# Float32r pairs against scaled fp16 pairs in a fused latent-attention layer: scores, queries, latent and feed-forward products

## The reference

```python
xn = _layernorm(x)
q = (xn @ wq).reshape(b, s, 16, 192)                 # 128 plain and 64 rotary columns per head
kva = xn @ wkv_a                                     # 128 latent and 64 rotary columns
ckv = ckv * rsqrt(mean(ckv * ckv) + 1e-6) * kv_norm_scale
kv = (ckv @ wkv_b).reshape(b, s, 16, 256)            # 128 key and 128 value columns per head
q_pe, k_pe = _rope(q_pe, cos, sin), _rope(k_pe, cos, sin)
scores = einsum('bhqd,bhkd->bhqk', qs, ks) * 192 ** -0.5     # causal
out = softmax(scores) @ v @ wo
x = x + out + einsum('btd,rde->bte', xn, factors) / sqrt(8) + bias
```

## Time and profile before

| | |
|---|---|
| median of 3 runs | 1624.83 us (1623.87 to 1628.01) |
| profiled execution, its own time | 1624.0 us |
| its span in the profile | 1622.2 us |
| TensorE busy, share of the span | 1578.3 us, 97% |
| VectorE | 984.7 us, 61% |
| ScalarE | 875.5 us, 54% |
| GpSimd | 902.1 us, 56% |
| granted TensorE clock, mean | 0.992 |

### The profile page before, as it was taken

One profiled execution on the slowest core, in us unless ns is written; L12 is line 12 of the kernel. 1 busy time (PEld: TensorE's weight loads), 2 busy tenths in 40 slices (PEclk: granted clock), 3 DMA queues, 4 the chain that ended last, 5 costly groups with the idle time before them and its releaser, 6 DMA issues.

```text
span 1622.2 us, 24924 instructions
## 1 busy us (share of the span) xinstructions
PE 1578.3 (97%) x7856; PEld 1198.7 (74%) x7856; DVE 984.7 (61%) x2286; ACT 875.5 (54%) x2264; POOL 902.1 (56%) x856
## 2 busy tenths in 40 slices
PE   5789999999999999999999999999999999999998
PEld 5667777777777777677777777777777777778786
DVE  6765666566666655655555555555656656665766
ACT  4554555555555556556555555555535555543554
POOL 3664556455555555555655655566645555563553
PEclk9899999999999999999999999999999999999999
DMA  8855878878787879778888778787957778865675
GB/s 279 307 127 120 172 164 166 178 149 178 149 167 164 162 177 225 154 174 167 165 179 163 152 150 164 167 209 160 242 131 166 165 167 169 216 166 123 168 177 127
DMA packets 646882, 280.23 MB, mean 173 GB/s; under 512 B 599392, under 2 KB 612192, under 8 KB 645344
## 3 DMA queue, kind: packets, MB, share of 16 engines
q1 hardware_dynamic: 646752, 278.63, 76.7%
HBM read 102.37 MB, written 33.55 MB: 84 GB/s over the span
## 4 chain that ended last, share of the span: by engine, by line
PE 92%; DVE 3%; ACT 2%; POOL 1%; issue 1%; DMA 1%; SPq 0%; ACTq 0%; POOLq 0%; DVEq 0%
PE ps L318 18%; PE ps L320 17%; PE ps L319 17%; PE ps L442 8%; PE ps L447 8%; PE ps L448 8%; PE ps L444 8%; PE ps L443 8%; POOL q L1022 1%; ACT ex L622 1%; DVE kt L803 1%; DMA wsq<-wq_in 0%; PE ps L337 0%; DMA st<-x_in 0%; DVE acc L896 0%
## 5 line engine op out<-in xcount | busy, mean ns | idle before, releaser
L1031 POOL TENSOR_TENSOR st<-ex,st 128x512 f16<-128x512 f32 (+3 forms) x640 | 639.7, 1020 | 617.6 <-ACT st L632 613.1
L622 ACT ACTIVATE ex<-ps,nm 128x512 f32<-128x512 f32 (+3 forms) x640 | 395.4, 621 | 639.8 <-DVE nm L869 639.8
L632 ACT ACTIVATE st<-ex 128x512 f16<-128x512 f32 (+3 forms) x640 | 344.5, 566 | 6.4 <-ACT ex L622 0.8
L853 DVE TENSOR_REDUCE gm<-ps 128x1 f32<-128x512 f32 (+1 forms) x384 | 248.8, 667 | 130.4 <-PE ps L448 130.1
L442 PE MATMUL ps<-kTh,q 128*128 128x512 f32 (+3 forms) x640 | 250.0, 391 | 4.2 <-DVE kRl L817 3.8
L447 PE MATMUL ps<-kRh,q 128*128 128x512 f32 (+3 forms) x640 | 232.8, 364 | 4.9 <-POOL q L1022 4.9
L444 PE MATMUL ps<-kTh,q 128*128 128x512 f32 (+3 forms) x640 | 232.3, 363 | 0.0
L443 PE MATMUL ps<-kTl,q 128*128 128x512 f32 (+3 forms) x640 | 231.7, 362 | 0.0
L448 PE MATMUL ps<-kRl,q 128*128 128x512 f32 (+3 forms) x640 | 231.7, 362 | 0.0
L318 PE MATMUL ps<-pT,vH 128*128 128x512 f16 (+3 forms) x640 | 223.5, 349 | 0.0
L319 PE MATMUL ps<-pT,vH 128*128 128x512 f16 (+3 forms) x640 | 222.1, 347 | 0.0
(11 more groups left out here) (144 smaller groups left out, 2446.4 us busy)
## 6 DMA issues: line engine op xcount, KB each, us to landing
wA<-w_abs SPq DMA_DIRECT2D x48, 512.0 KB, 3.8
wV<-w_vo SPq DMA_DIRECT2D x48, 512.0 KB, 3.7
wP<-w_pe SPq DMA_DIRECT2D x24, 512.0 KB, 4.1
pT<-st SPq DMA_TRANSPOSE x640, 3.3
w_abs<-wA SPq DMA_DIRECT2D x16, 512.0 KB, 2.9
w_vo<-wV SPq DMA_DIRECT2D x16, 512.0 KB, 3.0
x_t<-early SPq DMA_DIRECT2D x3, 2048.0 KB, 8.5
xT<-x_t SPq DMA_DIRECT2D x6, 1024.0 KB, 7.6
```

The source lines that it names most:

```text
L622: e.activation(ex[:, n % NEX, 0:keys], s_bank(n)[:, 0:keys], ACT.Exp, bias=nm[:, (i * QT + r) % 4:(i * QT + r) % 4 + 1], scale=SCALE, accu ...
L632: e.activation(stage(n, keys)[:, :, 0, :], ex[:, n % NEX, 0:keys].rearrange("p (t n) -> p t n", n=P), ACT.Copy).then_inc(z["a_pH"], 1)
L853: e.tensor_reduce(m, b, AX_X, ALU.max).then_inc(z["v_max"], 1)
L1031: e.tensor_tensor(s[:, :, 1, :], ex[:, n % NEX, 0:keys].rearrange("p (t n) -> p t n", n=P), s[:, :, 0, :], ALU.subtract).then_inc(z["g_pL" ...
```

## The change

- The parts of x, W_abs, the rotary weights, the latent weights, the keys, the queries and the factor sum become fp16 instead of float32r. The transposes, the product W_abs itself, W_vo and the output product stay float32r or float32.
- So that small low parts are not lost in fp16, operands carry powers of two: x by 2^10 (through the normalisation), keys by 2^12 (through the latent scale), queries are multiplied by 2^-14 when they are read from PSUM (L605: `scale=BACK`, an immediate), the rotary tables by 2^-14 on the host.
- Each pair of heads gets a weight scale of its own, worked out on the chip (`squares`, `scale_pair`): VectorE squares and sums Wq (1024 columns), the rotary weights (512) and Wk (256) of two heads, TensorE adds the partitions with a matrix of ones (`nrm`, 4 columns), VectorE makes a reciprocal square root out of an integer formula and from it four columns of `scales`. The latent weights (`nra`) and the factor sum (`nrf`) get one each.
- The scale of the exponentials (L622) was the immediate `SCALE` and is now the pointer `scales[:, pair(i), 2:3]`; likewise in `row_max`, `w_pe`, `w_abs`, the latent and feed-forward products.
- Order: `squares(i + 2)` in r0 of even units up to 12, `scale_pair(i + 2)` and the rotary weights' high part in r1, their low part in r2. `nrm` takes a bank in the turn, right ahead of `tq`. Key and value weights now have buffers and loads of their own, two heads at once. The factor sum is squared in r0 of unit 0, split in r1, and its eight feed-forward tiles lie in r2 and r3 instead of in r0 to r3; the bias is added by GpSimd within unit 0.
- Stores and reloads of W_abs, the rotary weights, x and the factor sum have half the bytes.

The diff, cut to its core:

```diff
-HEADROOM = float(np.log(32.0))
+XS, KS, WS, PS, BACK = 2.0 ** 10, 2.0 ** 12, 2.0 ** 15, 2.0 ** 15, 2.0 ** -14
+HEADROOM = float(np.log(PS))
...
     if r == 0:
-        for e in range(2, H, 2):
-            if i == max(0, e - 3):
-                out.append(("wpe", e))
         if 1 <= i <= H:
             out.append(("wo", i - 1))
         if i + 1 < NU:
             out.append(("q", i + 1))
-        if i + 2 <= H + 2:
-            out.append(("skv", i + 2))
+        if 3 <= i + 2 <= H + 2:
+            out.append(("sv", i + 2))
+        if i % 2 == 0 and i + 2 < H:
+            out.append(("sq", i + 2))
+        if i == 0:
+            out.append(("sqf", 0))
...
-    if i == 0:
-        out += [("ffn", n) for n in range(2 * QT) if min((n + 1) // 2, 3) == r]
+    if i == 0 and r >= 2:
+        out += [("ffn", n) for n in range((r - 2) * QT, (r - 1) * QT)]
...
     if r == 1:
+        if i % 2 == 0 and i + 2 < H:
+            out += [("nrm", i + 2), ("wpe", i + 2)]
+        if i == 0:
+            out.append(("nf", 0))
...
-IN_BANKS = ("q", "pe", "tkv", "wvo", "tq", "wabs", "out", "ffn")
+IN_BANKS = ("q", "pe", "tkv", "wvo", "tq", "wabs", "out", "ffn", "nrm", "nf")
...
-        kTh = sb("kTh", [P, S], F32R)
+        kTh = sb("kTh", [P, S], F16)
...
             def wq_transpose(h):
                 b = free_bank(("tq", h))
-                e.wait_ge(z["d_wq"], 16 * (h + 1))
+
+                e.wait_ge(z["v_sq"], h // 2 + 1)
...
+            def norm(key, ready, columns):
+
+                b = free_bank(key)
+                e.wait_ge(z[ready], count(key))
+                e.matmul(b[:, 0:columns.shape[-1]], ones[:, :], columns, start=True, stop=True).then_inc(
+                    z["p_" + key[0]], 1)
...
-                             bias=nm[:, (i * QT + r) % 4:(i * QT + r) % 4 + 1], scale=SCALE,
+                             bias=nm[:, (i * QT + r) % 4:(i * QT + r) % 4 + 1], scale=scales[:, pair(i), 2:3],
                              accum_out=ssum[:, i % 2, r, p:p + 1]).then_inc(z["a_exp"], 1)
...
+            def factors_high():
+                e.wait_ge(z["v_fsc"], 1)
+                e.activation(ff[:, 0, :, :], fsum, ACT.Identity, bias=eps[:, 2:3], scale=fsc[:, 1:2]).then_inc(
+                    z["a_ff"], 1)
...
+            def square_sum(w, at, n, total):
+                return e.tensor_tensor_reduce(out=sqr[:, at:at + n], in0=w, in1=w, scale=1.0, scalar=0.0, op0=ALU.mult,
+                                              op1=ALU.add, accum_out=total)
...
+            def squares(i):
+
+                e.wait_ge(z["d_wk"], 16 * (i + 2))
+                e.tensor_tensor(wsk[:, :, :], wsk[:, :, :], scl[:, 0:1].unsqueeze(2).broadcast_to([P, 2, P]),
+                                ALU.mult).then_inc(z["v_sk"], 1)
...
+                square_sum(wsq[:, :, :, :].rearrange("p a k n -> p (a k n)"), 0, 2 * E, nrm[:, 0:1])
+                e.wait_ge(z["d_wp"], 64 * (i // 2 + 1))
+                square_sum(wsp[:, :, :].rearrange("p k n -> p (k n)"), 2 * E, E, nrm[:, 1:2])
+                e.wait_ge(z["v_sk"], i // 2 + 1)
+                square_sum(wsk[:, :, :].rearrange("p a n -> p (a n)"), 3 * E, 2 * P, nrm[:, 2:3]).then_inc(z["v_sq"], 1)
...
             def q_latent(i):
                 e.wait_ge(z["a_q"], i + 1)
-                e.tensor_tensor(q[:, i % 2, 1, :], bank(("q", i)), f(q[:, i % 2, 0, :]), ALU.subtract).then_inc(
-                    z["v_q"], 1)
+                e.scalar_tensor_tensor(out=q[:, i % 2, 1, :], in0=bank(("q", i)), scalar=BACK, in1=q[:, i % 2, 0, :],
+                                       op0=ALU.mult, op1=ALU.subtract).then_inc(z["v_q"], 1)
...
-            for k4 in range(KE):
-                e.wait_ge(z["a_ff"], k4 + 1)
-                e.tensor_tensor(ff[:, 1, k4, :], fsum[k4], f(ff[:, 0, k4, :]), ALU.subtract).then_inc(z["v_ff"], 1)
```

More of the change, by code:

```diff
@@ L115, in fills @@
             out.append(("parts", i + 1))
+    if r == 2 and i % 2 == 0 and i + 2 < H:
+        out.append(("wpe_low", i + 2))
     for e in range(2, NU, 2):
@@ L127, in fills @@
             out.append(("parts", i + 1))
+    if i == 0:
+        out += [("bias", n) for n in range(2 * QT) if min((n + 1) // 3, 2) == r]
+    for k in range(2, NC):
+        if i == k * H + 1:
+            out.append(("bias", k * QT + r))
     return out
-IN_BANKS = ("q", "pe", "tkv", "wvo", "tq", "wabs", "out", "ffn")
+IN_BANKS = ("q", "pe", "tkv", "wvo", "tq", "wabs", "out", "ffn", "nrm", "nf")
 def bank_order():
-    pre = [("tq", 0), ("tkv", 0)]
+    pre = []
     for t in range(NT + 4):
@@ L322, in count @@
             def count(key):
-                return key[1] // 2 + 1 if key[0] == "pe" else key[1] + 1
+                return key[1] // 2 + 1 if key[0] in ("pe", "nrm") else key[1] + 1
             def free_bank(key):
@@ L593, in w_pe @@
                     e.wait_ge(z["d_sP"], 16 * (i // 2))
-                e.activation(by4(wP[:, 0, :]), wsp[:, :, :], ACT.Copy).then_inc(z["a_wpe"], 1)
+                e.activation(by4(wP[:, 0, :]), wsp[:, :, :], ACT.Identity, bias=eps[:, 2:3],
+                             scale=scales[:, i // 2, 1:2]).then_inc(z["a_wpe"], 1)
             def w_o(h):
@@ L868, in row_max @@
                     e.wait_ge(z["a_exp"], rows_done(R - 4))
-                e.scalar_tensor_tensor(out=nm[:, R % 4:R % 4 + 1], in0=m, scalar=-SCALE, in1=head[:, 0:1],
+                if i < H and r == 0:
+                    e.wait_ge(z["v_scale"], i // 2 + 1)
+                e.scalar_tensor_tensor(out=nm[:, R % 4:R % 4 + 1], in0=m, scalar=scales[:, pair(i), 3:4], in1=head[:, 0:1],
                                        op0=ALU.mult, op1=ALU.add).then_inc(z["v_nm"], 1)
@@ L1222, in _ @@
             load_wo(0)
-            load_wkv(2)
-            load_wq(2)
+            for m in range(2, 4):
+                load_wk(m)
+                load_wq(m)
+            load_wp(2)
+            load_wv(3)
             store_abs(0)
```

363 lines of the change are left out of this document (224 added, 139 removed).

## The result

The changed kernel takes 1650.38 us (1646.57 to 1651.71, four runs) against 1624.35 for the kernel before: ratio 1.0153, 95% interval 1.0128 to 1.0177, so 26 us slower. The forecast was 1638 (1622 to 1652 for its own case, 1606 to 1664 in all). The profiled execution took 1651.7 us with a span of 1649.8, 27.6 more than the span before. One execution of each of two later runs took far longer than all others (3208 us with the pointer in the kernel before, 2258 us with the factor in the queries) and is left out of their ratios.

The account below looks back on a forecast made before the run. TensorE was taken as the bound, with little to spare. Terms -69 + 45 + 7 + 16.5 + 13.7 + 1 = +14 on 1624.0 us gave 1638 us (1622 to 1652 for its own case, 1606 to 1664 in all).

Parts of the forecast that it names:

- The even units of chunk 3: Units 2 to 12: squares on VectorE and a bank wait stall TensorE 7.5 us in each of six: 45 us.
- Both waits: Even units of chunk 3: r1's bias waits behind squares, then the key transpose for the bank of r1's output product.
- The pace: TensorE: 512-column score products step at 0.2164 us instead of 0.233; with other products 69 us off, if nobody waits.
- rival (d): The pace comes with what is streamed, not with the type; the 69 us stays: 1707 us. Chance 0.03.
- The pointer: A second pointer adds 0.09 us to each of 640 exponentials; 13.7 us in chunk 2 and units 14, 15, 16, 31.
- Rival (a): The second pointer costs nothing in an exponential, being fetched beside the first: 1618 us. Chance 0.14.
- Unit 0: Squares, factor work and later feed-forward tiles make unit 0 13 us longer; as a stall 16.5 us.
- The startup: First 88 us: VectorE, the bound, gets 6 us more work but no longer stands 4.4 for a weight load: +1.
- The clock: TensorE's granted clock falls after the gaps in six even units of chunk 3: 1.2 us per unit, 7 us.
- rival (c): Lower clock for all values products of six units and in unit 0, GpSimd holds sums: 25 more, 1663 us. Chance 0.18.
- Rival (b): The bank wait does not bite as written; only the pointers bind: 1574 us. Chance 0.06.
- (e): Squares at the lower bound (1.3 us) and no clock loss: 21 us less, 1617 us. Chance 0.07.

Follow-up runs that it names:

- The constant: Changed kernel with one constant for all pairs, instead of a pointer, in the exponentials and the bias: 1626.78 us, 23.6 less.
- the run that isolates it: Changed kernel with squares on ScalarE, norm product back in the turn of the three banks: 1621.23 us, 22 more than with it out of the turn.

## Why the prediction was right, point by point

**The even units of chunk 3** carried it. For unit 4 the steps were: bias of r1 at 18.55 us, measured 18.94 (276.46 + 0.22 - 257.74); key transpose released at 19.3, measured 19.66; r2 at 22.8 and 1.2 for the clock, 24.0 together, measured 25.15; the unit near 44, measured 45.7, and 47.0 for unit 2. The squares were priced at 2.6 + 0.3 and took 3.3. Both waits were where the order blocks had put them, and the runs show each. The helper product out of the turn and the squares on ScalarE together give back 44.0 us in the six units (274.5 to 230.4). The bank wait is 14.9 of them if it is taken out first and 23.2 if it is taken out last, the squares 29.1 or 20.8: the two overlap, and no single share belongs to either. In all 48.7 us, where the steps (45 + 7, less 1.4 of pace per unit) give 44.

**The pace.** Right in its size where nothing waits: odd units of chunk 3 lose 1.36 each, those of chunk 2 1.0. The type of the operands does it. The rule of the Trainium skill that the prediction cites ("TensorE: Matmul & The Clock Gate", back-to-back issue gap), which names no type and which the page calls the gap of an isolated matmul, would have made this term zero. The run with float32r decides against it: 0.231 with that type, 0.216 with fp16, in the same kernel. That refutes rival (d) too. The step that booked 69 us as if all arrived was too kind. Of the 47 us that the scores make, 30 arrived.

**The pointer** was the step that failed most. I put 13.7 us on it outside units 0 to 12 and wrote that chunks 1 and 0 have over 1.5 us to spare and get the pace in full. Chunk 1 did (12.1 us); chunk 0 did not. The constant gives back 24, some 22 of them outside units 0 to 12 and 9 in chunk 0 and at the end, where a later row meets GpSimd and the bias takes 1.16 us. The 1.25 per even unit of chunk 2 was too much: the terms that I listed, with the 0.35 us that the earlier trace rows leave, add up to 1.1, and the constant gives back 0.8. The 0.09 us per exponential was right (0.088). Rival (a), that it is free, is refuted.

**Unit 0**: +13 forecast, +10.1 measured. ScalarE's squares give 6.4 of these back; the feed-forward tiles in r2 and r3 alone were not tried. The startup was 2.4 shorter, not 1 longer; it differs by up to 3 us between runs whose startup is the same code, so this says little.

**The clock**: 7 us for six units was about right for the part behind one gap (seven products at 0.43 in unit 6 are 1.5), and rival (c), all fifteen at the lower level, did not come. The other half of (c), sums held by GpSimd, came in part: 1024 elements took 1.95 and 512 took 1.14, 3.3 us for all three with the reads. Rival (b), the bank wait not biting, is refuted by the run that isolates it, and (e), squares at 1.3 us and no clock loss, by these rows and by the clock.

**The sum** was 12 us low: some 5 in the even units, 9 in chunk 0 and the end, 3 in units 14 to 16, less 3 in unit 0 and 3 in the startup; about 1 is not assigned. The measured time lies 1.6 us under the upper end of the forecast's own range. It lies inside partly by luck: the terms booked too low make 17 us together, and two that erred the other way, one of them the startup, which varies by itself, took back 6. By the prediction's own prices (a) with (e) would also be 1597, not the 1606 that it gives as its lower end.

## What to carry to other kernels

A faster type for the engine that bounds a kernel pays only where no chain is as long as that engine's work: measure each kind of stage for its own slack, by the idle time ahead of the product and at every piece, before the gain is booked. When a small helper product is added, look at what it does to the turn of the banks: four columns in the turn cost 1.3 to 3.9 us per unit, according to where the squares were, and all of that went once they were written into the free end of another product's bank. When two waits stand one behind the other, take each out first and last: their shares differ. Put added sums on an engine that waits at that moment and that a running GpSimd operation doesn't hold up (ScalarE here). Keep a per-group scale out of the operation that runs 640 times: in the operand that is made 64 times it cost 0.3 us in an even unit of chunk 2 instead of 0.8.

## What the runs showed of the hardware that I had not expected

- The same gap of TensorE (3.24 us) was followed by four products at 1.2 GHz in one unit and by ten in another of the same execution, a difference of 1.3 us per unit.
- A fused square and sum on VectorE with both inputs in SBUF took 0.41 us for 256 elements in one place and 1.36 beside GpSimd, longer by what was left of GpSimd's operation. ScalarE took 1.06 for 1024 elements with GpSimd busy throughout, and 0.51 for the 256 (its scale is a pointer; GpSimd was idle then).
- float32r has no single pace: products of 512 columns step at 0.233 to 0.235 us in the kernel before and at 0.231 in the changed kernel with the score operands in float32r. Why it differs is open.
- Slower products made the even units 50 to 62 shorter by 0.3 us on average, while fewer biases of chunk 0 took over 0.5 us (3 for 13). That the one is the cause of the other was not tried by itself.
